# A recurrence of sigmoids cut into chunks of ten tokens: three column chains in place of two halves, fewer filler matmuls, a first sweep that begins a token later

## The chip, the cores and the metric

One core of one Trainium2 chip. Times are microseconds of the device for one launch, median of several runs; lower is better.

## The reference, cut to what matters

The model is a graph convolution block, an attention layer and a recurrent layer on 32 batches, 32 channels and 400 tokens. The change touches only the recurrent layer at the end:

```python
Wx = ((flat - mean) * rsqrt(var + 1e-5) * gamma + beta)      # normalised over all batches and tokens
Vt = V.T                                                     # V is 32x32 and orthogonal (from a QR)
def step(yt, wx_t):
    yt = sigmoid(wx_t + yt @ Vt)
    return (yt, yt)
y0 = zeros((B, H))
_, ys = lax.scan(step, y0, swapaxes(Wx, 0, 1))               # 400 tokens, one after the other
t = t + swapaxes(ys, 0, 1)
```

`gamma` and `beta` are drawn with a spread; everything is float32.

## The kernel before, in words

Layout. Four batches of 32 channels fill the 128 partitions, and there are G = 8 such groups, so a value of one token is 128 partitions x 8 columns. Matmul weights are block diagonal.

The recurrence is not run through 400 tokens. The sequence is cut into NC = 40 chunks of L = 10 tokens, and all chunks run side by side: one step takes token s of every chunk, 8 x 40 = 320 columns. A first sweep starts every chunk from a state of zero; since a state of zero needs no matmul, its first token is a sigmoid alone, and SKIP = 1 leaves out token 0, so it covers tokens 1 to 9. Its last states, moved by one chunk (`chain`, L833), start the second sweep of ten steps, which gives the output. A test (L881 to L890) then compares the last states of the two sweeps: if any of them differs by more than 2^-18 (MEET is its square), 39 further sweeps run. The profile shows none.

Within a sweep the 320 columns go as two halves h of 160 columns (groups 0 to 3 and 4 to 7), so that one half's matmul runs beside the other's sigmoid. For each step and half:

- VectorE has put `scl * ul + shf` (the normalised input) into a slot of PSUM ahead of time (`seed`, L829: 2 or 3 steps of one half in one instruction). PLACES = 9 slots for each half lie three to a bank in banks 4h to 4h+2.
- TensorE adds V to it (L1183; a float32 matmul is two pairs of LDWEIGHTS and MATMUL), and then runs a filler, a bf16 matmul of 256 columns into an unused bank (`fill`, L1173).
- ScalarE takes the sigmoid from the slot to `yb` (L587), which is the input of the next matmul of that half.

Each engine takes its instructions in program order, and on each the halves alternate: h0, h1, h0, h1. The semaphores are `seeded` (VectorE to TensorE), `pre` (TensorE to ScalarE), `y_ok` (ScalarE to TensorE and VectorE).

Ahead of the first step: the statistics over all tokens end with a small float32 matmul (L1176), two small ScalarE instructions (L579, L581), a table load for the sigmoid (L584), and `scl` and `shf` on VectorE (L822, L823). Beside them TensorE writes six banks once, so that the steps' matmuls can accumulate (`prime`, L1168, 480 columns each), and runs FILLS_FIRST = 10 fillers. The first token's sigmoid (L598) reads `ul` with `scl` and `shf` as scale and bias.

Between the sweeps VectorE moves the states (L836, once for each half), then copies the last states for the test (L852, all 320 columns), and ScalarE waits for this copy before the second sweep. During the second sweep VectorE adds the residual for each token in turn (L869, 320 columns), and seeds the slot of token 9 after token 3's sigmoid. The last token is added by halves (L874), and after each half SyncE issues two output DMAs of 400 KB (L339).

Of the kernel before, what the change touches and what calls it, by code (L numbers as in the profile page):

```python
# [42 lines left out]
NC = N // L  # L43
PLACES = 9
SKIP = 1
FILL = 256
FILLS_FIRST = 10
COLS = G * NC
HALF = COLS // 2
FULL = N // P  # L50
# [31 lines left out]
def build(nc, x_tok, x, consts, out):  # L82
    with ExitStack() as ctx:
# [16 lines left out]
        ka, kb, qa, qb = ([sb(f"{name}{h}", [P, NB, N], BF16) for h in range(2)] for name in ("ka", "kb", "qa", "qb"))  # L100
        ul = sb("ul", [P, 2, L, G // 2, NC])
        yb = sb("yb", [P, L + 1, G, NC])
# [56 lines left out]
        def col(n, w=1, rows=P):  # L159
# [4 lines left out]
        bn_s2, bn_h2 = col(19, 3), col(22, 3)  # L164
        mv, tot, nvar, lnv, rsv, scl, shf, okc = (
            col(25, 2), col(27, 2), *(col(n) for n in range(29, 35)))
        S_GC, S_Z, S_POST = 0, 1, 2
# [29 lines left out]
            sem(n) for n in ("bn_c", "bn_pe", "bn_act", "primed", "cmp_c", "cmp_pe", "flag_ok", "added"))  # L197
        start_ok = [sem("start_ok0"), sem("start_ok1")]
        seeded = [sem("seeded0"), sem("seeded1")]
        pre = [sem("pre0"), sem("pre1")]  # L200
        y_ok = [sem("y_ok0"), sem("y_ok1")]

# [3 lines left out]
        CREDIT_DMA = 16  # L206
        OUT_G = 2
        LOADED = 14 * 16
        WARM_FIRST, WARM = 10, 2
        SLOT = HALF  # L210
        PRIMED = 3 * SLOT
        PRIME_ORDER = (0, 4, 1, 5, 2, 6)
        FILL_BANK, SMALL_BANK = 3, 7
        LAST_STEP_ADDS = L + 1

# [12 lines left out]

        def step_slot(h, p):

            return ps[:, 4 * h + p // 3, SLOT * (p % 3):SLOT * (p % 3 + 1)]

        def seed_count(sweep, s):

            return s // 3 + 1 + (PLACES // 3 + 1) * sweep - 1 if sweep else (s - SKIP - 1) // 3 + 1

        def y_half(h, s):

            return yb[:, s, 4 * h:4 * h + 4, :].rearrange("p g c -> p (g c)")

# [28 lines left out]
        def _(sp):  # L269
# [65 lines left out]
            def store_output(sums):  # L335
                for h in range(2):
                    sp.wait_ge(added, LAST_STEP_ADDS * (sums - 1) + L + h)
                    for g in range(4 * h, 4 * h + 4, OUT_G):
                        sp.dma_start(out[g:g + OUT_G].rearrange("g p n -> p g n"),  # L339
                                     outs[:, g:g + OUT_G, :]).then_inc(out_done, 16)  # L340
                sp.wait_ge(out_done, 16 * (G // OUT_G) * sums)

# [57 lines left out]
        def _(act):  # L400
# [185 lines left out]
            def step(h, sweep, s):  # L586
                nc.scalar.activation(y_half(h, s + 1), step_slot(h, place(sweep, s)), ACT.Sigmoid).then_inc(y_ok[h], 1)  # L587
# [12 lines left out]
            for s in range(SKIP + 1, L):  # L600
                for h in range(2):
                    act.wait_ge(pre[h], s - SKIP)
                    step(h, 0, s)
# [9 lines left out]
        def _(dve):  # L613
# [150 lines left out]
            def project2(g, banks=NORM_BANKS):  # L764
                dve.wait_ge(wx_done, g + 1)
                dve.wait_ge(rs2_ready, g + 1)
                nc.vector.tensor_tensor(ul[:, g // 4, :, g % 4, :],  # L767
                                        ps[:, banks[1], 0:N].rearrange("p (c s) -> p s c", s=L),
                                        rs2.rearrange("p (c s) -> p s c", s=L), ALU.mult).then_inc(u2_ready, 1)

            def stats(g):
                dve.wait_ge(u2_ready, g + 1)
                nc.vector.bn_stats(stat[:, g, :], ul[:, g // 4, :, g % 4, :]).then_inc(stat_ready, 1)

# [32 lines left out]
            def blink(ins):  # L807
# [15 lines left out]
            blink(nc.vector.scalar_tensor_tensor(out=shf, in0=tot[:, 0:1], scalar=scl, in1=c_("beta"),  # L823
                                                 op0=ALU.mult, op1=ALU.add))

            def seed(h, sweep, lo, hi):

                o = SLOT * (place(sweep, lo) % 3)
                nc.vector.tensor_scalar(ps[:, 4 * h + place(sweep, lo) // 3, o:o + SLOT * (hi - lo)],  # L829
                                        ul[:, h, lo:hi, :, :].rearrange("p s g c -> p (s g c)"),  # L830
                                        scl, shf, ALU.mult, ALU.add).then_inc(seeded[h], 1)

            def chain(h, base):  # L833

                dve.wait_ge(y_ok[h], base)
                nc.vector.tensor_copy(yb[:, 0, 4 * h:4 * h + 4, 1:NC],  # L836
                                      yb[:, L, 4 * h:4 * h + 4, 0:NC - 1]).then_inc(start_ok[h], 1)

            FIRST = ((SKIP + 1, SKIP + 4), (SKIP + 4, SKIP + 7), (SKIP + 7, L))
            LATER = ((0, 3), (3, 6), (6, 9))  # L840

            for lo, hi in FIRST:
                for h in range(2):
                    dve.wait_ge(primed, 1 + PRIME_ORDER.index(4 * h + place(0, lo) // 3))
                    seed(h, 0, lo, hi)
            for lo, hi in LATER[:-1]:
                for h in range(2):
                    dve.wait_ge(y_ok[h], hi + 1)
                    seed(h, 1, lo, hi)
            for h in range(2):  # L850
                chain(h, L - SKIP)
            nc.vector.tensor_copy(ys, yb[:, L, :, :]).then_inc(cmp_c, 1)  # L852
            for h in range(2):
                seed(h, 1, *LATER[-1])

            def last_seeds(base):

                for h in range(2):
                    dve.wait_ge(y_ok[h], base + 3)
                    seed(h, 1, PLACES, L)  # L860

            def add_residual(base, seeding=False):

                for j in range(L - 1):
                    if seeding and j == 3:
                        last_seeds(base)
                    for h in range(2):
# [4 lines left out]
                for h in range(2):  # L872
                    dve.wait_ge(y_ok[h], base + L)
                    nc.vector.tensor_tensor(by_step(outs[:, 4 * h:4 * h + 4, :], L - 1),  # L874
                                            by_step(t0[:, 4 * h:4 * h + 4, :], L - 1),
                                            y_half(h, L), ALU.add).then_inc(added, 1)

# [12 lines left out]
            with dve.If(dve.value_load(flag[0:1, 0:1], min_val=0, max_val=1) != 0):  # L890
                with dve.Fori(0, NC - 1) as k:
                    for h in range(2):
# [4 lines left out]
                for h in range(2):  # L897
                    dve.wait_ge(y_ok[h], 2 * L - SKIP + L * (NC - 1))
                dve.wait_ge(out_done, 16 * (G // OUT_G))
                add_residual(2 * L - SKIP + L * (NC - 2))  # L900
# [3 lines left out]
        def _(pe):  # L904
# [277 lines left out]
            def step(h, sweep, s):  # L1182
                mm_(step_slot(h, place(sweep, s)), c_("vT"), y_half(h, s), start=False, stop=True,  # L1183
                    skip_group_check=True).then_inc(pre[h], 1)
                fill()

            def steps(sweep):
                for s in range(L):
                    for h in range(2):
                        pe.wait_ge(seeded[h], seed_count(1, s) + (PLACES // 3 + 1) * (sweep - 1))  # L1190
                        if s == 0:
# [5 lines left out]
            for s in range(SKIP + 1, L):  # L1197
                for h in range(2):
                    pe.wait_ge(seeded[h], seed_count(0, s))
# [111 lines left out]
```

## Time and profile before

| what | us |
|---|---|
| median of 3 runs | 222.96 (222.94 to 223.4) |
| span of the profiled execution | 221.9 |
| mean granted TensorE clock over it | 0.966 |
| the recurrence's first matmul starts, in that span | 195.38 |
| its last pair of matmuls ends | 213.97 |
| first output DMA is issued | 214.51 |

The span runs from the first instruction of the program to the last; the launch's own time for that one execution is not given, and the median of the runs is 1.0 above the span. In the profile PE is TensorE's matmuls, PEld its weight loads, DVE VectorE, ACT ScalarE, SP SyncE (SPq its issuing of DMAs). The end of a matmul is modelled, its start is not. PEclk is the granted TensorE clock: 1.00 is 2.4 GHz, 0.50 is 1.2 GHz.

### The profile page before, as it was taken

The page shows a single profiled execution, that of the slowest core. Times are in us where ns is not written, and L with a number is a line of the kernel's source. Part 1 is how long each engine was busy: PE and PEld are TensorE (multiplying, and loading weights), DVE is VectorE, ACT ScalarE, POOL GpSimd, SP SyncE. Part 2 cuts the span into 40 slices and gives each one's busy share as a digit, 9 for nine tenths or more (in the row PEclk, how much of TensorE's full clock was granted, in tenths as well). Part 3 has the DMA queues.
Part 4 walks back from the last instruction along what each step waited for, and adds up shares of the span by engine and source line. Part 5 has one row for each costly group of instructions (what it writes and reads, how often), then busy time and mean ns, then how long its engine had stood idle before and what let it go on. Part 6 is the DMA issues. An engine that isn't in the chain of part 4 may idle for free. (4 is left out here: it accounts for less than half of the span.)

```text
span 221.9 us, 3477 instructions
## 1 busy us (share of the span) xinstructions
PE 198.5 (89%) x1182; PEld 97.9 (44%) x1182; DVE 161.2 (73%) x294; ACT 169.1 (76%) x307; POOL 29.8 (13%) x44
## 2 busy tenths in 40 slices
PE   6858999999999869699999999999999997699950
PEld 6733655646546335123243434334343332376630
DVE  0559289989989926978685777859596865765980
ACT  4083798799599799988989989898989954445630
POOL 7000000450330160432020000101010000000000
PEclk9999999999999999979999999999999999579995
DMA  6940200357348050880627162443500000000016
GB/s 183 370 149 15 74 1 0 98 220 200 123 150 219 20 222 3 273 194 6 167 58 190 38 155 71 117 111 85 140 0 3 0 0 0 3 3 0 0 65 234
DMA packets 20229, 21.95 MB, mean 99 GB/s; under 512 B 2062, under 2 KB 17102, under 8 KB 20084
## 3 DMA queue, kind: packets, MB, share of 16 engines
q1 hardware_dynamic: 20212, 21.73, 33.5%
q8 instruction: 10, 0.16, 0.3%
q14 instruction: 7, 0.06, 0.1%
HBM read 14.74 MB, written 6.96 MB: 98 GB/s over the span
## 5 line engine op out<-in xcount | busy, mean ns | idle before, releaser
L508 ACT ACTIVATE arena<-ps 128x800 f32<-128x800 f32 (+1 forms) x56 | 44.6, 798 | 5.8 <-PE ps L1066 5.3
L515 ACT ACTIVATE arena<-arena 128x800 f32<-128x800 f32 (+1 forms) x56 | 46.5, 831 | 0.0
L1066 PE MATMUL ps<-qa,ka 128*128 128x400 bf16 (+1 forms) x128 | 35.4, 340 | 2.0 <-ACT arena L508 1.9
L1066 PE MATMUL ps<-qb,kb 96*128 96x400 bf16 (+1 forms) x128 | 35.4, 338 | 0.0
L742 DVE TENSOR_TENSOR psum<-arena 128x400 f32<-128x400 f32 x32 | 19.6, 612 | 14.3 <-ACT arena L515 14.3
L742 DVE TENSOR_TENSOR psum<-psum,arena 128x400 f32<-128x400 f32 x32 | 19.5, 608 | 6.0 <-ACT arena L515 4.6
L1066 PEld LDWEIGHTS ps<-qa,ka 128*128 128x128 bf16 (+1 forms) x128 | 10.4, 97 | 26.1 <-ACT arena L508 13.7
L1099 PE MATMUL ps<-arena,vb 128*32 128x400 f32 x192 | 21.6, 527 | 0.3 <-issue 0.3
L751 DVE RECIPROCAL arena<-ps 128x400 f32<-128x400 f32 x7 | 18.5, 2650 | 0.0
L661 DVE COPY arena<-arena 32x400 f32<-32x400 f32 x48 | 17.2, 358 | 0.9
L587 ACT ACTIVATE yb<-ps 128x160 f32<-128x160 f32 x36 | 10.9, 303 | 9.1 <-PE ps L1183 6.8
L1183 PE MATMUL ps<-yb,cst 128*128 128x160 f32 x72 | 17.1, 332 | 0.0
L967 PE MATMUL ps<-arena,cst 128*128 128x400 f32 x32 | 13.0, 528 | 3.3 <-DVE arena L661 3.3
L368 POOL TENSOR_TENSOR arena<-arena,cst 128x400 bf16<-128x400 f32 x4 | 5.0, 1248 | 71.5 <-ACT arena L476 61.7
L1066 PEld LDWEIGHTS ps<-qb,kb 96*128 96x128 bf16 (+1 forms) x128 | 10.4, 98 | 9.2 <-issue 5.2
L1183 PEld LDWEIGHTS ps<-yb,cst 128*128 128x128 f32 x72 | 11.2, 196 | 5.8 <-issue 4.0
L378 POOL COPY vb<-vst 128x384 f32 (+1 forms) x8 | 4.8, 595 | 60.9 <-PE ps L1095 60.9
L1173 PE MATMUL ps<-ka 128*128 128x256 bf16 x46 | 12.3, 308 | 0.0
L829 DVE TENSOR_SCALAR ps<-ul,small 128x480 f32<-128x480 f32 (+2 forms) x14 | 9.0, 702 | 3.6 <-ACT yb L587 3.6
L702 DVE TENSOR_TENSOR arena<-arena 128x400 bf16<-128x400 f32 x16 | 11.2, 741 | 0.0
L421 ACT ACTIVATE arena<-ps,small 96x400 f32<-96x400 f32 (+1 forms) x16 | 10.5, 675 | 0.9 <-PE ps L958 0.7
L679 DVE TENSOR_TENSOR arena<-ps,arena 128x400 f32<-128x400 f32 x8 | 4.2, 568 | 8.8 <-ACT arena L454 8.8
(148 smaller groups left out, 360.9 us busy)
## 6 DMA issues: line engine op xcount, KB each, us to landing
ka<-dk SPq DMA_DIRECT2D x32, 100.0 KB
qa<-dq SPq DMA_DIRECT2D x32, 100.0 KB
dk<-arena SPq DMA_DIRECT2D x8, 300.0 KB, 2.2
dq<-arena SPq DMA_DIRECT2D x8, 300.0 KB, 2.6
arena<-x_tok SPq DMA_DIRECT2D x4, 400.0 KB
t<-x SPq DMA_DIRECT2D x1, 1600.0 KB, 11.4
kb<-dk SPq DMA_DIRECT2D x16, 100.0 KB
qb<-dq SPq DMA_DIRECT2D x16, 100.0 KB
```

The costliest lines, as they stand in the source:

```text
L508: nc.scalar.activation(prob[par][:, lo:hi, :], ps[:, o:o + hi - lo, 0:N], ACT.Exp, scale=2.0).then_inc(e1_done, 1)
L515: nc.scalar.activation(p, p, ACT.Exp).then_inc(p_ready, 1)
L587: nc.scalar.activation(y_half(h, s + 1), step_slot(h, place(sweep, s)), ACT.Sigmoid).then_inc(y_ok[h], 1)
L661: last = nc.vector.tensor_copy(*tap_input(par, j, k))
L702: nc.vector.tensor_tensor(p[par][:, slots[2], :], r[par], p[par][:, slots[1], :], ALU.subtract).then_inc(parts_ready, 1)
L742: nc.vector.tensor_tensor(dst, a, prob[par][:, t, :], ALU.add).then_inc(part_sum, 1)
L751: nc.vector.reciprocal(rden, ps[:, 5, 0:N]).then_inc(rden_ready, 1)
L967: mm_(ps[:, 2 * par + 1, 0:N], cst[:, o + P * j:o + P * j + P], tap_in[par][j], start=(j == 0), stop=False)
L1066: last = mm_(ps[row:row + keys, bank, 0:N], kk[par][0:rows, b, o:o + keys], qq[par][0:rows, b, :], start=first, stop=not first, skip_group ...
L1099: mm_(ps[C * b:C * b + C, 4, 0:N], vb[:, par, P * k + C * b:P * k + C * b + C], prob[par][:, FULL * b + k, :], start=(k == 0), stop=False, ...
L1173: mm_(ps[:, FILL_BANK, 0:FILL], ka[0][:, 0, 0:P], ka[0][:, 0, 0:FILL], start=True, stop=True)
L1183: mm_(step_slot(h, place(sweep, s)), c_("vT"), y_half(h, s), start=False, stop=True, skip_group_check=True).then_inc(pre[h], 1)
```

## The change

The columns of the recurrence go as three chains of 3, 3 and 2 groups, that is 120, 120 and 80 columns, and every loop over h has three members. Each chain has two banks (2h and 2h+1) with four slots each (ROOM), PLACES = 8 slots in all; seeds are for 4 steps of one chain (2 or 3 at a sweep's end). The filler after each step's matmul goes, and of the ten fillers in front three stay. The first sweep starts at token 2 (SKIP = 2) from states of 0.5: an added float32 matmul of one column (V times ones) ahead of L1176 and an added VectorE instruction give the bias `shf_first = shf + 0.5 * V 1` for its first sigmoid. The output goes as three DMAs (600, 600, 400 KB) in place of four. The scaled input `ul` is laid out by token, group, chunk.

```diff
-PLACES = 9
-SKIP = 1
+PLACES = 8
+ROOM = 4
+SKIP = 2
-FILLS_FIRST = 10
+FILLS_FIRST = 3
-HALF = COLS // 2
+CHAINS = ((0, 3), (3, 6), (6, 8))
+WIDE = 3 * NC
-        PRIME_ORDER = (0, 4, 1, 5, 2, 6)
+        PRIMED = ROOM * WIDE
+        PRIME_ORDER = (0, 2, 4, 1, 3, 5)
 # SyncE
-                for h in range(2):
+                for h, (lo, hi) in enumerate(CHAINS):
                     sp.wait_ge(added, LAST_STEP_ADDS * (sums - 1) + L + h)
-                    for g in range(4 * h, 4 * h + 4, OUT_G):
-                        sp.dma_start(out[g:g + OUT_G].rearrange("g p n -> p g n"),
-                                     outs[:, g:g + OUT_G, :]).then_inc(out_done, 16)
+                    sp.dma_start(out[lo:hi].rearrange("g p n -> p g n"), outs[:, lo:hi, :]).then_inc(out_done, 16)
 # ScalarE
-            for h in range(2):
-                act.wait_ge(bn_c, 5)
-                nc.scalar.activation(y_half(h, SKIP + 1), ul[:, h, SKIP, :, :].rearrange("p g c -> p (g c)"),
-                                     ACT.Sigmoid, bias=shf, scale=scl).then_inc(y_ok[h], 1)
+            act.wait_ge(bn_c, 6)
+            for h, (lo, hi) in enumerate(CHAINS):
+                nc.scalar.activation(y_part(h, SKIP + 1), ul[:, SKIP, lo:hi, :].rearrange("p g c -> p (g c)"),
+                                     ACT.Sigmoid, bias=shf_first, scale=scl).then_inc(y_ok[h], 1)
 # VectorE
+            blink(nc.vector.scalar_tensor_tensor(out=shf_first, in0=ps[:, SMALL_BANK, 8:9], scalar=0.5, in1=shf,
+                                                 op0=ALU.mult, op1=ALU.add))
-            FIRST = ((SKIP + 1, SKIP + 4), (SKIP + 4, SKIP + 7), (SKIP + 7, L))
-            LATER = ((0, 3), (3, 6), (6, 9))
+            FIRST = ((SKIP + 1, SKIP + 1 + ROOM), (SKIP + 1 + ROOM, L))
+            LATER = ((0, ROOM), (ROOM, 2 * ROOM))
-            for lo, hi in LATER[:-1]:
-                for h in range(2):
-                    dve.wait_ge(y_ok[h], hi + 1)
-                    seed(h, 1, lo, hi)
+            for h in range(len(CHAINS)):
+                dve.wait_ge(y_ok[h], ROOM + 1)
+                seed(h, 1, *LATER[0])
 ...
-                    if seeding and j == 3:
+                    if seeding and j == ROOM:
                         last_seeds(base)
 # TensorE
+            mm_(ps[:, SMALL_BANK, 8:9], c_("vT"), c_("ones")[:, 0:1], start=True, stop=True)
             mm_(ps[:, SMALL_BANK, 0:2], c_("avg4"), mv, start=True, stop=True).then_inc(bn_pe, 1)
 ...
             def step(h, sweep, s):
-                mm_(step_slot(h, place(sweep, s)), c_("vT"), y_half(h, s), start=False, stop=True,
+                mm_(step_slot(h, place(sweep, s)), c_("vT"), y_part(h, s), start=False, stop=True,
                     skip_group_check=True).then_inc(pre[h], 1)
-                fill()
```

## Rows read from the trace of the kernel before

**Rows 1.** Chain of waits ahead of the first step: start us, us, what
```profile
193.46 2.13 PE ps L1173 x10
```
**Rows 2.** Timeline of TensorE, same stretch: start us, us, engine, line, operation, tiles, shapes
```profile
190.68 0.35 PE L1176 MATMUL ps<-small,cst 128*128 128x2 f32 x1
190.90 2.56 PE L1168 MATMUL ps<-ka 128*128 128x480 bf16 x6
...
195.38 0.47 PE L1183 MATMUL ps<-yb,cst 128*128 128x160 f32 x1
195.65 0.47 PE L1183 MATMUL ps<-yb,cst 128*128 128x160 f32 x1
```
**Rows 3.** Timeline of ScalarE and VectorE, same stretch
```profile
192.07 1.28 ACT L584 ACT_TABLE_LOAD   x1
192.35 0.22 DVE L823 SCALAR_TENSOR_TENSOR small<-small,cst 128x1 f32<-128x1 f32 x1
192.61 3.85 DVE L829 TENSOR_SCALAR ps<-ul,small 128x480 f32<-128x480 f32 x6
193.37 0.93 ACT L598 ACTIVATE yb<-ul,small 128x160 f32<-128x160 f32 x2
```
**Rows 4.** Groups by line, 189 to 222 us: count | busy us, mean ns | idle before, releaser
```profile
L829 DVE TENSOR_SCALAR ps<-ul,small 128x480 f32<-128x480 f32 x10 | 7.2, 774 | 3.6 <-ACT yb L587 3.6
```
**Rows 5.** Timeline, one cycle of h0 in the second sweep
```profile
206.04 0.30 PEld L1183 LDWEIGHTS ps<-yb,cst 128*128 128x128 f32 x2 [0.23 <-issue]
206.61 0.30 ACT L587 ACTIVATE yb<-ps 128x160 f32<-128x160 f32 x1 [0.27 <-PE ps L1183]
207.03 0.30 PEld L1183 LDWEIGHTS ps<-yb,cst 128*128 128x128 f32 x2 [0.23 <-issue]
```
**Rows 6.** Timeline, output DMAs, and two steps ahead of them on VectorE
```profile
213.41 0.73 DVE L869 TENSOR_TENSOR outs<-t,yb 128x320 f32<-128x320 f32 x1 [0.25 <-ACT yb L587]
214.06 0.77 DVE L874 TENSOR_TENSOR outs<-t,yb 128x160 f32<-128x160 f32 x2
214.51 2.59 SPq L339 DMA_DIRECT2D out<-outs  x4
```
**Rows 7.** Busy time: PE, PEld, DVE, ACT, POOL, PEclk, DMA share, GB/s
```profile
219.00:219.50 0.50, 0.00 (x0) 0.00 (x0) 0.00 (x0) 0.00 (x0) 0.00 (x0) 0.50 1.03 394
```
**Rows 8.** Timeline, h0's pairs: tokens 3 and 9 of sweep one, 1 and 9 of sweep two
```profile
196.72 0.44 PE L1183 MATMUL ps<-yb,cst 128*128 128x160 f32 x2
202.69 0.30 PE L1183 MATMUL ps<-yb,cst 128*128 128x160 f32 x1
205.07 0.37 PE L1183 MATMUL ps<-yb,cst 128*128 128x160 f32 x1
213.03 0.37 PE L1183 MATMUL ps<-yb,cst 128*128 128x160 f32 x1
```
**Rows 9.** Timeline of ScalarE: one activation at two widths
```profile
174.34 0.84 ACT L508 ACTIVATE arena<-ps 128x800 f32<-128x800 f32 x1
...
176.19 0.50 ACT L508 ACTIVATE arena<-ps 128x400 f32<-128x400 f32 x1 [0.25 <-PE ps L1066]
```
**Rows 10.** Timeline, two float32 matmuls of 128 columns in a stream
```profile
11.90 0.39 PE L1036 MATMUL ps<-cst 128*128 128x128 f32 x2
12.13 0.39 PE L1037 MATMUL ps<-cst 128*128 128x128 f32 x2
```
**Rows 11.** Timeline of VectorE between the sweeps
```profile
204.27 0.32 DVE L852 COPY ys<-yb 128x320 f32<-128x320 f32 x1
```
**Rows 12.** Busy time, columns as in rows 7, with the granted clock (PEclk)
```profile
80.50:83.90 3.40, 1.97 (x6) 1.24 (x7) 1.05 (x2) 3.00 (x6) 1.18 (x2) 1.00 0.11 37
186.30:189.70 3.40, 1.34 (x4) 0.40 (x3) 1.76 (x3) 1.13 (x2) 0.00 (x0) 1.00 0.00 0
189.70:193.10 3.40, 2.65 (x8) 1.31 (x9) 2.20 (x9) 1.53 (x3) 0.00 (x0) 0.50 0.01 2
193.10:196.50 3.40, 3.40 (x16) 2.57 (x15) 3.35 (x6) 1.49 (x4) 0.00 (x0) 0.50 0.01 2
```

More of the change, by code:

```diff
@@ L164, in build @@
         bn_s2, bn_h2 = col(19, 3), col(22, 3)
-        mv, tot, nvar, lnv, rsv, scl, shf, okc = (
-            col(25, 2), col(27, 2), *(col(n) for n in range(29, 35)))
+        mv, tot, nvar, lnv, rsv, scl, shf, okc, shf_first = (
+            col(25, 2), col(27, 2), *(col(n) for n in range(29, 36)))
         S_GC, S_Z, S_POST = 0, 1, 2
@@ L197, in build @@
             sem(n) for n in ("bn_c", "bn_pe", "bn_act", "primed", "cmp_c", "cmp_pe", "flag_ok", "added"))
[L198 to L201, printed above, removed]
+        start_ok = [sem(f"start_ok{h}") for h in range(len(CHAINS))]
+        seeded = [sem(f"seeded{h}") for h in range(len(CHAINS))]
+        pre = [sem(f"pre{h}") for h in range(len(CHAINS))]
+        y_ok = [sem(f"y_ok{h}") for h in range(len(CHAINS))]
         CREDIT = 2
@@ L227, in place, with step_slot, y_part @@
             return s - SKIP - 1 if sweep == 0 else s % PLACES
-        def step_slot(h, p):
-            return ps[:, 4 * h + p // 3, SLOT * (p % 3):SLOT * (p % 3 + 1)]
+        def step_slot(h, p, steps=1):
+            width = (CHAINS[h][1] - CHAINS[h][0]) * NC
+            return ps[:, 2 * h + p // ROOM, width * (p % ROOM):width * (p % ROOM + steps)]
         def seed_count(sweep, s):
-            return s // 3 + 1 + (PLACES // 3 + 1) * sweep - 1 if sweep else (s - SKIP - 1) // 3 + 1
-        def y_half(h, s):
-            return yb[:, s, 4 * h:4 * h + 4, :].rearrange("p g c -> p (g c)")
+            return s // ROOM + (PLACES // ROOM + 1) * sweep if sweep else (s - SKIP - 1) // ROOM + 1
+        def y_part(h, s):
+            return yb[:, s, CHAINS[h][0]:CHAINS[h][1], :].rearrange("p g c -> p (g c)")
         def apart(eng):
@@ L824, in _ @@
                                                  op0=ALU.mult, op1=ALU.add))
+            blink(nc.vector.scalar_tensor_tensor(out=shf_first, in0=ps[:, SMALL_BANK, 8:9], scalar=0.5, in1=shf,
+                                                 op0=ALU.mult, op1=ALU.add))
             def seed(h, sweep, lo, hi):
[L828 to L830 removed]
+                nc.vector.tensor_scalar(step_slot(h, place(sweep, lo), hi - lo).rearrange("p (s n) -> p s n", s=hi - lo),
+                                        ul[:, lo:hi, CHAINS[h][0]:CHAINS[h][1], :].rearrange("p s g c -> p s (g c)"),
@@ L842, in _ @@
+            FIRST = ((SKIP + 1, SKIP + 1 + ROOM), (SKIP + 1 + ROOM, L))
+            LATER = ((0, ROOM), (ROOM, 2 * ROOM))
             for lo, hi in FIRST:
-                for h in range(2):
-                    dve.wait_ge(primed, 1 + PRIME_ORDER.index(4 * h + place(0, lo) // 3))
+                for h in range(len(CHAINS)):
+                    dve.wait_ge(primed, 1 + PRIME_ORDER.index(2 * h + place(0, lo) // ROOM))
                     seed(h, 0, lo, hi)
-            for lo, hi in LATER[:-1]:
-                for h in range(2):
-                    dve.wait_ge(y_ok[h], hi + 1)
-                    seed(h, 1, lo, hi)
@@ L850, in _ @@
-            for h in range(2):
+            for h in range(len(CHAINS)):
+                dve.wait_ge(y_ok[h], ROOM + 1)
+                seed(h, 1, *LATER[0])
+            for h in range(len(CHAINS)):
                 chain(h, L - SKIP)
             nc.vector.tensor_copy(ys, yb[:, L, :, :]).then_inc(cmp_c, 1)
-            for h in range(2):
-                seed(h, 1, *LATER[-1])
+            for h in range(len(CHAINS)):
+                seed(h, 1, *LATER[1])
             def last_seeds(base):
-                for h in range(2):
-                    dve.wait_ge(y_ok[h], base + 3)
+                for h in range(len(CHAINS)):
+                    dve.wait_ge(y_ok[h], base + ROOM)
@@ L864, in add_residual @@
                 for j in range(L - 1):
-                    if seeding and j == 3:
+                    if seeding and j == ROOM:
                         last_seeds(base)
-                    for h in range(2):
+                    for h in range(len(CHAINS)):
                         dve.wait_ge(y_ok[h], base + j + 1)
@@ L871, in add_residual @@
                                             ALU.add).then_inc(added, 1)
-                for h in range(2):
+                for h, (lo, hi) in enumerate(CHAINS):
                     dve.wait_ge(y_ok[h], base + L)
-                    nc.vector.tensor_tensor(by_step(outs[:, 4 * h:4 * h + 4, :], L - 1),
-                                            by_step(t0[:, 4 * h:4 * h + 4, :], L - 1),
-                                            y_half(h, L), ALU.add).then_inc(added, 1)
+                    nc.vector.tensor_tensor(by_step(outs[:, lo:hi, :], L - 1), by_step(t0[:, lo:hi, :], L - 1),
+                                            y_part(h, L), ALU.add).then_inc(added, 1)
             add_residual(L - SKIP, seeding=True)
@@ L891, in _ @@
                 with dve.Fori(0, NC - 1) as k:
-                    for h in range(2):
+                    for h in range(len(CHAINS)):
                         chain(h, 2 * L - SKIP + L * k)
@@ L896, in _ @@
                     last_seeds(2 * L - SKIP + L * k)
-                for h in range(2):
+                for h in range(len(CHAINS)):
                     dve.wait_ge(y_ok[h], 2 * L - SKIP + L * (NC - 1))
-                dve.wait_ge(out_done, 16 * (G // OUT_G))
+                dve.wait_ge(out_done, 16 * len(CHAINS))
                 add_residual(2 * L - SKIP + L * (NC - 2))
@@ L1182, in step @@
             def step(h, sweep, s):
-                mm_(step_slot(h, place(sweep, s)), c_("vT"), y_half(h, s), start=False, stop=True,
+                mm_(step_slot(h, place(sweep, s)), c_("vT"), y_part(h, s), start=False, stop=True,
                     skip_group_check=True).then_inc(pre[h], 1)
-                fill()
             def steps(sweep):
                 for s in range(L):
-                    for h in range(2):
-                        pe.wait_ge(seeded[h], seed_count(1, s) + (PLACES // 3 + 1) * (sweep - 1))
+                    for h in range(len(CHAINS)):
+                        pe.wait_ge(seeded[h], seed_count(1, s) + (PLACES // ROOM + 1) * (sweep - 1))
                         if s == 0:
@@ L1197, in _ @@
             for s in range(SKIP + 1, L):
-                for h in range(2):
+                for h in range(len(CHAINS)):
                     pe.wait_ge(seeded[h], seed_count(0, s))
```

23 lines of the change are left out of this document (10 added, 13 removed).

## The prediction

> **What bounds the kernel now.** I read the chain of waits first, then the timeline along it, then busy time by stretch for the clock and the DMAs. Ahead of the first step the chain runs through TensorE's fillers [rows 1]. The timelines [rows 2, 3] show that this is padding: h0's first sigmoid begins at 193.37 and ends near 193.9 (two overlap in 0.93), its seed is done at 192.61 + 0.77 = 193.38 [rows 4], yet its first matmul starts at 195.38, after ten fillers. So 1.4 us of the front is filler on the path.
>
> In the steps nobody is full; each half is bound by its own round trip [rows 5]: weight load at 206.04, both matmuls, sigmoid at 206.61 (0.57 after the load) for 0.30, next weight load at 207.03 (0.12 after its end). Sum 0.99. The fillers lie in the gaps. Eighteen such steps run: eight in the first sweep, ten in the second.
>
> The end is DMA: the first of four is issued at 214.51 [rows 6], and while they run the DMA share is 1.03 at 394 GB/s [rows 7]. 1.64 MB at this rate is 4.2 us of the 7.4 from the first issue to the span's end; the rest is start, landing and closing. So what counts is when the first output DMA is issued.
>
> **The change part by part.** I follow chain 0 against h0 by the start of its pairs: 195.38 for token 2, 196.72 for token 3, 202.69 for token 9, then 205.07 and 213.03 for tokens 1 and 9 of the second sweep [rows 2, 8].
>
> *Front, later part.* The added float32 matmul (V times ones) stands ahead of L1176, which everything behind waits for. One MATMUL of L1176 starts at 190.68 and the next instruction's at 190.90 [rows 2]: 0.22 each at the half clock, two of them 0.44. That goes on the path: statistics, two small activations, table load and sigmoids all start 0.44 later. Bounds: 0, were it started earlier than the wait lets it, and 0.58, both matmuls unpipelined. The added VectorE instruction, 0.22 like L823 plus a gap of 0.04, ends inside the table load of 1.28 [rows 3] and costs the sigmoid nothing; the seeds begin 0.26 later beyond the 0.44, at 193.31.
>
> *Front, earlier part.* The table load then ends at 193.80. The first sigmoid with 120 columns takes 0.51 less 0.03 (40 columns at 0.85 ns: 400 columns more cost L508 0.84 - 0.50 [rows 9]) and ends at 194.28. Chain 0's seed (480 columns, 0.77) ends at 194.08. TensorE's primes end near 193.7 and three fillers at 0.213 each (2.13 for ten [rows 1]) near 194.3: still hidden. Weight load 0.12 after the sigmoid, so the first pair starts at about 194.45, for token 3.
>
> *Half-clock steps.* Chains 1 and 2 wait for their seeds (194.8, 195.3), and at half clock two 120-column float32 MATMULs and loads take about 0.22 each, 0.43 per pair: three pairs make a step of 1.28. Walking them through: pairs start at 194.45, 194.9 and 195.4. Chain 0's first pair is through at about 195.1 (0.23 to the second MATMUL, 0.2 of columns, 0.2 of drain), its sigmoid at 195.4, but chain 2's pair holds TensorE until 195.85, where chain 0's token 4 starts. That pair ends at 196.45, the sigmoid at 196.77, and as the clock returns at 196.5 as now, token 5 starts at 196.92. Now h0's token 5 starts two steps of 0.995 after 196.72, at 198.71. Ahead: 1.79. In it are the token no longer computed (about 1.0 to 1.3), the fillers, and the 0.44 lost.
>
> *Warm steps.* With 120 columns a round trip loses 40 columns in the second matmul and in the sigmoid. A float32 MATMUL takes two cycles a column (160 columns in the 0.27 from 195.38 to 195.65, at 1.2 GHz [rows 2]), so 40 are 0.033 at 2.4 GHz; the sigmoid's 40 are 0.033. The first matmul I let save nothing, since the second waits for its own weights (0.03 more if it does save). 0.995 - 0.066 = 0.93. Does it fit? TensorE: in a stream, pairs of 128 columns start 0.23 apart [rows 10], and I take the same for 120 and 80, since loads set it: three make 0.69. ScalarE: 0.27 + 0.27 + 0.24 = 0.78 without overlap. Both are under 0.93, so the latency still binds. A price by columns alone would make the three 0.53, which changes nothing. Bounds for a step: 0.86 (the 80-column trip, if it could lead) and 1.00 (the wider interleaving costs what the columns save); I take 0.93, the arithmetic above. Four steps to token 9 of the first sweep save 0.25: ahead by 2.04. Eight steps in the second save 0.50.
>
> *Between the sweeps.* h0 needs 2.38 from token 9 to token 1, of which about 0.2 is the state copy and 0.2 ScalarE's wait for the 320-column copy of 0.32 [rows 11]. With three chains that copy stands behind three state copies, and the last of these waits for chain 2's last sigmoid. Chain 0's pair for token 9 starts at 200.65, its sigmoid ends at 201.43, those of chains 1 and 2 at 201.86 and 202.03. State copies of 0.2 end at 201.66, 202.09 and 202.28, the copy of all columns at about 202.52. Chain 0's next pair starts at 201.81 and is through at 202.3; its sigmoid waits until 202.55, and the sigmoids of chains 1 and 2, queued behind it, are due at 202.76 and 203.0 and lose nothing. So 1.16 to the first pair and 1.16 to the second, 2.32, ahead by 2.10, with the eight steps 2.60. Bounds: 2.0 and 2.9.
>
> The seeds for tokens 0 to 3 now wait for chain 0's fifth sigmoid (198.6) and end by 200.6, ahead of their use at 201.8: nothing.
>
> *VectorE behind it* is the engine that could come late. Six seeds run in 3.85 [rows 3], 0.64 each in mean, so three make 1.9; four additions of 0.65 (213.41 to 214.06 [rows 6]) 2.6; the last seeds 1.2. From the copy's end, 202.5, this ends near 208.2; chain 0 needs its slot for token 8 at 209.5. 1.3 us to spare, so nothing.
>
> *End.* Now from h0's last pair to the first DMA it is 1.48. The full-width addition for token 8 waits for the last chain, then 0.65, then chain 0's own addition of 0.38 (0.42 less 40 columns): 1.37. Ahead by 2.7. The output's bytes are the same and each engine of the DMA is full, so three issues for four gain 0 (0.2 at most).
>
> Sum: 195.38 to 194.45 and on, in all 2.7. The profiled span of 221.94 becomes 219.2; the median lies 1.0 above the span, which surrounds both: 222.96 - 2.7 = **220.3**.
>
> **The clock** is what I trust least, because what fed TensorE in the gaps is removed. In the trace the granted clock fell to 0.50 at 189.7, after 3.4 us in which PE was busy for 1.34, and stayed there over the next stretch, busy for 2.65; it rose at 196.5, after a stretch in which it was busy throughout [rows 12]. From 80.5 to 83.9 it was busy for 1.97 and the clock stayed at 1.00. After the change the steps at full clock hold 0.53 us of columns in 0.93 (320 columns, two MATMULs of two cycles), plus loads and drains; in the stretch ahead of 196.5 the primes, three fillers and the cold pairs leave gaps of perhaps 0.3 us. I expect the clock to come back and to stay.
> The Trainium skill speaks against the change here: "TensorE: Matmul & The Clock Gate", section "A second HAM failure mode: psum-queue depth-cycling", tells of a kernel whose TensorE paused briefly between groups of matmuls often enough that its clock went back and forth between the two levels. By that rule the steps here would run at 1.2 GHz in part or throughout; by the row from 80.5 they would not. It is the first rival.
>
> **Rivals.**
> 1. *The clock doesn't come back, or falls in the steps.* For it: the filler went from every gap, and the stretch of 2.65 busy did not raise the clock. Against: the row from 80.5, and cold pairs fill TensorE nearly wholly. Price: at half clock a step is set by three pairs of 0.43, 1.28 in place of 0.93. For 14 steps that is 4.9: 225.2, slower than before. It decides once more than 8 of the steps are cold (8 x 0.35 = 2.8). Chance 0.15. If the rise comes only one such stretch later (2.7 steps, 0.95): 221.3, chance 0.10.
> 2. *Three chains don't fit.* In-order engines alternate three, and TensorE's queue must pass a wait, two loads and two matmuls for each; were it 1.0 per step, 12 warm steps lose 0.07 each: 221.2. For it: a load is issued 0.12 after its sigmoid even now. Chance 0.09.
> 3. *The test between the sweeps fails.* Taking the reference's recurrence on its own inputs in double precision, the largest difference of a chunk's last state between the sweeps is 1.2e-6 now; with eight tokens from 0.5 it is 3.0e-6, against the limit of 2^-18 = 3.8e-6. It passes with a fifth to spare. Otherwise 39 sweeps of 9.7 follow, 380 us: 600. Chance 0.03.
>
> **How the numbers follow.** The forecast's own case has 0.63, from 219.6 to 221.0: the added matmul's bounds (-0.4, +0.1), the step between 0.90 and 0.96 (12 x 0.03 = 0.4 each way), the copies 0.3. With the delayed clock and rival 2 the range is 219.5 to 222.3; it leaves out the cold clock and the failed test, 0.18, and a little below. A measurement tells 0.2%, 0.45 us, from nothing. Faster: 0.63 + 0.10 + 0.09, less 0.04 for combinations of them: 0.78. Slower: 0.15 + 0.03 = 0.18. Same: 0.04.
>
> **What would show it.** PEclk 1.00 from about 196.5 until the last pair. First pair of the recurrence near 194.4, for a table load ending near 193.8. Chain 0's pairs 0.93 apart, TensorE's loads in groups of six. First output DMA near 211.8, with the DMA share at 1.0 behind it. Wrong: clock at 0.50 in the steps, pairs at 1.0 apart or more, VectorE's last seeds later than the matmul that waits for them, or instructions of the 39 further sweeps.

## The result, and the profile after

The changed kernel takes 221.73 us in the median of 20 executions (220.54 to 223.88), the kernel before 223.00 in 20 beside it (221.42 to 225.61). The ratio is 0.9944, interval 0.9917 to 0.9971: 1.3 us faster by the medians, where 2.7 was forecast. A second set, of 6 executions of the changed kernel and 23 of the kernel before, gave 221.43 against 223.70, ratio 0.990 (0.9847 to 0.9952): 2.3 faster by the medians. Both kernels vary from execution to execution by 1% and more; the ratios leave out executions more than 1.5% above a kernel's fastest, most of them of the kernel before, so they can understate the gain. The means of the first set are 223.30 and 221.86, of the second 223.68 and 221.54. Over all 112 executions of the kernel before and all 26 of the changed one, which were not all made side by side, they are 223.68 and 221.79: 1.9 apart.

The profiled execution of the changed kernel has a span of 219.2 and took 221.07. The 39 further sweeps did not run.

The chain of waits ahead of the first step (start us, us, what) has lost its primes and fillers [rows 1]; it now goes through the table load and the first sigmoid:

```profile
190.73 0.38 PE ps L1174 x2
191.11 0.24 PE ps L1175 x2
...
192.37 1.28 ACT L583
193.66 0.49 ACT yb L597
```

TensorE's timeline answers to [rows 2]. Its clock is at 2.4 GHz here: the primes take 1.38 for six (2.56 before), and TensorE then waits 1.40 for the sigmoid:

```profile
190.97 0.36 PE L1175 MATMUL ps<-small,cst 128*128 128x2 f32 x2
191.19 1.38 PE L1166 MATMUL ps<-ka 128*128 128x480 bf16 x6
192.41 0.49 PE L1171 MATMUL ps<-ka 128*128 128x256 bf16 x3
194.29 6.41 PE L1182 MATMUL ps<-yb,cst 128*128 128x120 f32 x33 [1.40 <-ACT yb L597]
```

Busy time by stretch (PE, PEld, DVE, ACT, POOL, PEclk, DMA share, GB/s) answers to [rows 12]. The clock did not fall ahead of L1175; it fell at 196.3, inside the steps, and came back at 199.7 (PEclk, the last number but two):

```profile
189.50:192.80 3.30, 2.07 (x13) 1.25 (x13) 2.12 (x8) 0.93 (x3) 0.00 (x0) 1.00 0.00 0
192.80:196.20 3.40, 2.00 (x13) 1.58 (x12) 3.33 (x8) 3.09 (x9) 0.00 (x0) 1.00 0.02 5
196.20:199.60 3.40, 3.40 (x18) 3.40 (x17) 1.36 (x3) 1.96 (x8) 0.00 (x0) 0.51 0.02 5
206.00:209.40 3.40, 3.36 (x24) 2.87 (x23) 3.40 (x7) 2.49 (x12) 0.00 (x0) 1.00 0.00 0
```

Chain 0's pairs start 0.90 apart at full clock (206.72, 207.63, 208.53, 209.44, 210.34) and 1.33 and 1.28 apart between 196.3 and 199.7 (196.28, 197.61, 198.89). Between the sweeps and at the end the timeline has, against [rows 11, 6]:

```profile
201.74 0.68 DVE L837 COPY yb<-yb 128x117 f32<-128x117 f32 x3 [1.11 <-ACT yb L586]
202.34 0.32 DVE L851 COPY ys<-yb 128x320 f32<-128x320 f32 x1
202.69 0.68 ACT L586 ACTIVATE yb<-ps 128x120 f32<-128x120 f32 x3 [0.50 <-DVE ys L851]
...
207.42 0.52 DVE L829 TENSOR_SCALAR ps<-ul,small 128x240 f32<-128x240 f32 x1
207.85 0.43 DVE L829 TENSOR_SCALAR ps<-ul,small 128x160 f32<-128x160 f32 x1
...
210.76 0.72 DVE L868 TENSOR_TENSOR outs<-t,yb 128x320 f32<-128x320 f32 x1
211.39 0.82 DVE L873 TENSOR_TENSOR outs<-t,yb 128x120 f32<-128x120 f32 x3
211.77 2.03 SPq L339 DMA_DIRECT2D out<-outs  x3
```

The first output DMA (SPq, the issuing of DMAs), forecast at 211.8, is issued at 211.77, and the span, forecast at 219.2, is 219.2. So the two profiles differ by just the 2.7 of the forecast, and the medians of the first set by half of it. That is the question of the experiments.

### The profile page after: what moved, and what is told of

The parts are those of the page before. It is cut to its first block and busy times, and to the rows that moved or that the text cites. A ratio compares the mean times of both kernels' runs of the same rounds, so it can differ in the third digit from the quotient of the medians.

```text
span 219.2 us, 3489 instructions
## 1 busy us (share of the span) xinstructions
PE 193.8 (88%) x1171; PEld 98.4 (45%) x1171; DVE 160.7 (73%) x298; ACT 170.3 (78%) x323; POOL 29.8 (14%) x44
## 5 line engine op out<-in xcount | busy, mean ns | idle before, releaser
L1182 PE MATMUL ps<-yb,cst 128*128 128x120 f32 (+1 forms) x102 | 16.6, 309 | 1.7 <-ACT yb L597 1.4
L1182 PEld LDWEIGHTS ps<-yb,cst 128*128 128x128 f32 x102 | 14.7, 212 | 3.7 <-DVE ps L829 1.8
L586 ACT ACTIVATE yb<-ps 128x120 f32<-128x120 f32 (+1 forms) x51 | 11.9, 260 | 4.8 <-PE ps L1182 3.7
L438 ACT ACTIVATE t<-arena,small 128x400 f32<-128x400 f32 x8 | 4.8, 630 | 7.6 <-DVE arena L670 7.4
L416 ACT ACTIVATE arena<-ps,small 128x400 f32<-128x400 f32 x8 | 5.4, 685 | 6.6 <-PE ps L951 6.6
```

The lines of the kernel that those rows point to most:

```text
L586: nc.scalar.activation(y_part(h, s + 1), step_slot(h, place(sweep, s)), ACT.Sigmoid).then_inc(y_ok[h], 1)
L1182: mm_(step_slot(h, place(sweep, s)), c_("vT"), y_part(h, s), start=False, stop=True, skip_group_check=True).then_inc(pre[h], 1)
```

## The experiments

I split each profile at two marks: the start of the matmul of avg4 (L1176 before, L1175 after; here "the mark") and the first output DMA. In the first two profiles: start to mark 190.45 and 190.97, mark to DMA 24.06 and 20.80, DMA to end 7.43 and 7.43.

Each launch also gives the mean granted clock of its execution. Every profile has one stretch of half clock in the first part or the middle, mostly near 94 us, and one at the end. With these two alone the mean is 0.978 or more (0.98 to 0.987 in most); below that, there was a further stretch. The number does not say where it lay. The medians of the kernel before also differ from one set of executions to the next (223.00, 223.49, 223.70, 223.38, 224.31), so that kernels of different sets are best compared through the kernel before beside them.

**Both kernels again.** No edit.

> The kernel before, unchanged, for a second profile of it. Theory A (the two profiled executions were not typical ones: the half-clock stretches fall elsewhere from execution to execution): the time from L1176 to the first output DMA, 24.06 in the first profile, comes out otherwise here, by 0.5 or more, and with it the place where the granted clock is 0.50. Theory B (the profile of before was typical, and what is lost is lost in executions of the changed kernel that the one profile of it does not show): 24.0 to 24.1 again, clock at half from 189.7 to 196.5 again, and launch time minus span 1.0.

> The changed kernel, unchanged, for a second profile of it. Theory A: from L1176 to the first output DMA 21.05 was one draw; another place of the half-clock stretch gives 20.0 to 23. Theory B: 22 or more, with half clock in the steps for two stretches of 3.4 or more. A third theory, that the part ahead of L1176 (the same in both kernels) varies by a microsecond and hides the difference: the start of L1176 moves by 0.5 or more against 190.73.

Busy time of the kernel before in its second profile, mark to DMA in the first line:

```profile
191.44:213.54 22.10, 20.70 (x126) 14.00 (x126) 17.24 (x33) 13.66 (x41) 0.00 (x0) 1.00 0.01 1
188.10:191.40 3.30, 0.53 (x2) 0.00 (x0) 2.02 (x4) 1.03 (x2) 0.00 (x0) 1.00 0.00 0
```

and of the changed kernel:

```profile
191.74:212.51 20.77, 18.31 (x115) 15.51 (x114) 16.51 (x36) 14.63 (x57) 0.00 (x0) 0.92 0.01 2
193.60:197.00 3.40, 2.00 (x13) 1.61 (x12) 3.33 (x8) 3.08 (x9) 0.00 (x0) 1.00 0.02 5
197.00:200.40 3.40, 3.40 (x18) 3.40 (x18) 1.35 (x3) 1.92 (x8) 0.00 (x0) 0.50 0.02 5
```

TensorE in the second profile of the kernel before, ten fillers and the first pair of matmuls:

```profile
192.90 1.25 PE L1173 MATMUL ps<-ka 128*128 128x256 bf16 x10
194.82 0.51 PE L1183 MATMUL ps<-yb,cst 128*128 128x160 f32 x2 [0.67 <-ACT yb L598]
```

Theory A (another execution, another place of the half clock) holds for the kernel before: 22.10 at full clock, in place of 24.06 with half clock at 189.7 to 196.5. Its first profile had caught an execution that loses 1.96 there. The changed kernel shows 20.77 and its half clock in the same place again. Of the executions of the kernel before, 36 of 92 have a mean clock of 0.978 or more (222.63 in the mean; the other 56: 224.49); of the changed kernel 1 of 26. The 20 executions of the kernel before in the first set have no clock on record. The mark itself moved, too, to 191.44 and 191.74: the part ahead of it, to which the change adds only the 0.24 of the new matmul, varies by a microsecond and more (over all fourteen profiles from 190.45 to 192.59). The third theory, that this hides the difference, is true of single executions.

**The wait for the statistics filled, in both kernels.**

```diff
             project2(G - 1, LAST_BANKS[G - 1])
+            for _ in range(26):
+                mm_(ps[:, 4, 0:FILL], ka[0][:, 0, 0:P], ka[0][:, 0, 0:FILL], start=True, stop=True)
```

> The kernel before with 26 more fillers (256 columns, bf16) right behind the last projection, in the 2.8 us in which TensorE waits for the statistics. Theory A: the clock stays at 1.00 from there to the last step, primes and fillers run at 0.20 and 0.107, the first step starts as soon as the sigmoid is there (3.6 us after L1176 in place of 4.9), and L1176 to first DMA is 22.4. The median falls by the average cost of the half-clock stretches in the kernel before, 0.5 to 1.5 us, and the times of its runs lie closer together. Theory B: no stretch in before costs anything, the median moves by under 0.3.

> The changed kernel with the same 26 fillers in the same place. Theory A: L1176 to first DMA 19.8 to 20.0, and 2.3 to 2.6 below the kernel before with the same fillers; against the changed kernel 1 to 2 lower, since its steps pay for a half-clock stretch by 0.38 a step and nothing in them covers it. If in its steps, without fillers, the clock falls all the same: half clock in a stretch of 3.4 within the steps, 21 or more, and the gain stays at 1 us against the kernel before with the same fillers.

Kernel before, mark to DMA and the stretch ahead of the mark:

```profile
190.81:212.90 22.09, 20.70 (x127) 13.99 (x126) 17.26 (x33) 13.67 (x41) 0.00 (x0) 1.00 0.01 1
187.40:190.80 3.40, 3.40 (x28) 2.55 (x26) 2.03 (x4) 1.09 (x2) 0.00 (x0) 1.00 0.02 5
```

Changed kernel:

```profile
192.56:212.28 19.72, 17.03 (x115) 13.97 (x114) 16.57 (x36) 14.28 (x57) 0.00 (x0) 1.00 0.01 2
192.90:196.30 3.40, 2.00 (x13) 1.05 (x10) 2.53 (x8) 2.83 (x6) 0.00 (x0) 1.00 0.02 5
```

The kernel before: median 222.94 against 223.70, mean clock 0.978 or more in 9 of 12 executions, and 22.09 as expected of the full clock (22.4 was 0.3 too much). The changed kernel without half clock takes 19.72: that is its own price, 2.38 less than 22.10, and the half-clock stretch in its steps costs 20.77 - 19.72 = 1.05. Its median is 221.23 (6 executions), hardly below the 221.43 of the changed kernel beside it, where 1 to 2 less was expected. The mark lay late in its profile (192.56), and 3 of 6 still have a further stretch; how much each takes back is open.

**The fillers, one place at a time.** In this order:

```diff
 # changed kernel, ten in front
-FILLS_FIRST = 3
+FILLS_FIRST = 10
 # changed kernel, behind the step's matmul
+                fill()
 # kernel before, three in front
-FILLS_FIRST = 10
+FILLS_FIRST = 3
 # kernel before, behind the step's matmul
-                fill()
```

> The changed kernel with ten fillers in front in place of three, none behind steps. Theory C (the half-clock stretch in its steps, from 196.3 in its profile, comes from the 1.4 us in which TensorE now waits ahead of the first step, 192.9 to 194.3): the clock stays at 1.00 through the steps, L1175 to first DMA 19.7 to 19.9 in place of 20.8, the median about 1 lower. Rival D (it comes from the missing fillers behind the steps): the stretch is there as before, 20.8, median unmoved.

> The changed kernel with a filler behind each step's matmul again, three in front. Theory D: no half clock in the steps. Theory C: it comes all the same. Either way a full-clock step is then set by TensorE, three pairs of 0.223 and three fillers of 0.107, 0.99 in place of 0.90: 12 or more of them cost 1.1 to 1.4, L1175 to first DMA 21.0 without a half-clock stretch, 22 or more with one.

> The kernel before with three fillers in front in place of ten, a filler behind each step as it was. Theory C: the wait ahead of the first step now brings half clock into its steps in about every execution; steps at half clock 1.2 to 1.5 in place of 1.0 for one stretch, L1176 to first DMA 22.6 to 23.3 against 22.1. Rival D: the fillers behind steps keep the clock, 22.1, or less where the clock had fallen ahead of L1176 (24.06 becomes 22.9).

> The kernel before with no filler behind steps, ten in front. Theory C: clock as in the kernel before, steps 0.99 (0.96 where a filler had held up h1), L1176 to first DMA 22.0 to 22.1, median within 0.5 of the kernel before. Rival D: half clock in the steps in about every execution, 22.6 or more.

Mark to DMA in the four, in this order; of the first also the half clock, which here fell ahead of the mark:

```profile
192.48:213.81 21.33, 20.51 (x121) 16.54 (x121) 16.34 (x35) 14.68 (x57) 0.00 (x0) 0.87 0.01 2
191.30:194.70 3.40, 2.67 (x9) 1.59 (x10) 1.78 (x9) 1.11 (x3) 0.00 (x0) 0.50 0.00 0
194.70:198.10 3.40, 3.40 (x16) 2.43 (x15) 3.36 (x7) 1.92 (x5) 0.00 (x0) 0.50 0.02 5
```

```profile
190.95:211.54 20.59, 18.80 (x166) 16.95 (x165) 16.86 (x36) 16.05 (x57) 0.00 (x0) 1.00 0.01 2
```

```profile
190.84:212.90 22.06, 19.93 (x119) 13.30 (x119) 17.23 (x33) 13.63 (x41) 0.00 (x0) 1.00 0.00 1
```

```profile
191.46:214.20 22.74, 18.31 (x90) 13.02 (x90) 17.25 (x33) 13.13 (x41) 0.00 (x0) 0.92 0.01 1
192.60:196.00 3.40, 3.40 (x16) 2.38 (x15) 2.97 (x6) 2.44 (x5) 0.00 (x0) 0.50 0.02 5
```

Medians, with the ratio to the kernel before beside them and its interval:

| kernel | median | ratio | executions at 0.978 or more |
|---|---|---|---|
| changed | 221.73, 221.43 | 0.9944, 0.990 | 1 of 26 |
| changed, ten in front | 221.28 | 0.9931 (0.9893 to 0.9969) | 4 of 11 |
| changed, filler behind steps | 221.41 | 0.9932 (0.9895 to 0.9969) | 8 of 12 |
| before | 223.49, 223.70, 223.38, 224.31 | | 36 of 92 |
| before, three in front | 222.91 | 1.0042 (1.0003 to 1.0082) | 6 of 12 |
| before, none behind steps | 223.37 | 1.0036 (0.9997 to 1.0076) | 2 of 12 |

Neither theory C (the wait ahead of the first step loses the clock) nor D (the missing fillers behind the steps do) stands alone. With fillers behind the steps the most executions of the changed kernel are without a further stretch (8 of 12 against 1 of 26), with ten in front some (4 of 11); I cannot say more from eleven. In the kernel before three in front in place of ten take 22.06 in place of 22.10: at full clock seven fillers are worth 0.04. The ratio has that kernel 0.4% slower than the kernel before (1.0042), the means have it 0.1 us faster (223.50 against 223.60), so I read no difference from either. What theory D gains is paid back: in the changed kernel a step with three fillers is 0.94 to 0.95 in place of 0.90 (I had expected 0.99), and 20.59 is hardly less than 20.77.

The first and the last profile lost the clock in a third place. With ten in front, half clock lay over the primes, all ten fillers and the start of the first step, as in the first profile of the kernel before: the first pair starts 4.92 behind the mark in place of 3.32, and 21.33 is 1.6 more than 19.72. With none behind the steps it lay over the last two primes, the fillers and about half of the first step (first pair 3.90 behind the mark in place of 3.38, first step 1.23 in place of 1.00: 22.74). All its further steps, without any filler, ran at full clock and 1.00 apart, so steps of two halves without fillers do not by themselves lose it. The last count decides nothing: its profile has two more half-clock stretches, of 3.4 each, in the first 25 us, far ahead of the recurrence.

**The token and the chains, one at a time.** The kernel before with the first sweep from token 2 and states of 0.5; the changed kernel with it from token 1 and states of zero, the opposite edit.

```diff
-SKIP = 1
+SKIP = 2
 ...
-                act.wait_ge(bn_c, 5)
+                act.wait_ge(bn_c, 6)
-                                     ACT.Sigmoid, bias=shf, scale=scl).then_inc(y_ok[h], 1)
+                                     ACT.Sigmoid, bias=shf_first, scale=scl).then_inc(y_ok[h], 1)
+            blink(nc.vector.scalar_tensor_tensor(out=shf_first, in0=ps[:, SMALL_BANK, 8:9], scalar=0.5, in1=shf,
+                                                 op0=ALU.mult, op1=ALU.add))
+            mm_(ps[:, SMALL_BANK, 8:9], c_("vT"), c_("ones")[:, 0:1], start=True, stop=True)
```

> The kernel before with one part of the change alone: the first sweep starts at token 2 from 0.5, with the added matmul and bias; two halves, all fillers. Where no half-clock stretch falls behind L1176 the kernel before needs 22.10 from L1176 (the matmul of avg4) to the first output DMA; a step less takes 0.995; the added matmul lies ahead of that mark, so 21.1, and 0.22 to 0.26 is lost ahead of it (from the end of the statistics to the mark). Median 0.7 to 0.8 below the kernel before. A rival, that the clock lottery grows worse: median unmoved.

> The changed kernel without that part: three chains of 120, 120 and 80, three fillers in front and none behind steps, but the first sweep from token 1 and a state of zero. With no half-clock stretch L1176 to first output DMA is 19.72 (the changed kernel with the gap filled) plus 0.90, 20.6; with one stretch in the steps 21.7. Theory C/D (the missing fillers make such a stretch fall in about every execution): half clock in its steps in the profile, 21.7. Median 0.3 to 1.0 below the kernel before, by the columns and fillers alone.

The first: mark to DMA by busy time, and VectorE between the sweeps:

```profile
192.59:214.03 21.44, 19.67 (x122) 13.31 (x121) 16.82 (x34) 13.05 (x39) 0.00 (x0) 1.00 0.01 2
```

```profile
201.82 1.46 DVE L831 TENSOR_SCALAR ps<-ul,small 128x480 f32<-128x480 f32 x2 [1.53 <-ACT yb L587]
203.18 0.38 DVE L838 COPY yb<-yb 128x156 f32<-128x156 f32 x2
```

The second, mark to DMA, and its half clock in the steps:

```profile
191.63:213.19 21.56, 19.17 (x119) 16.62 (x119) 16.86 (x35) 15.65 (x60) 0.00 (x0) 0.92 0.01 2
197.20:200.60 3.40, 3.40 (x18) 3.40 (x17) 1.77 (x4) 2.01 (x9) 0.00 (x0) 0.50 0.02 5
```

One token less in two halves gives 0.66 (22.10 to 21.44), not 0.995: the second seeds (1.46) now stand ahead of the state copies on VectorE, and h0's trip between the sweeps is 1.63 in place of 1.27. In three chains the same token gives 0.79 (21.56 against 20.77, both with one half-clock stretch in the steps), nearer to the 0.90 of a step; between the sweeps chain 0's pairs are 1.18 apart in both, since only one bank of seeds stands there. The chains with their fewer fillers are worth 22.10 - 20.5 = 1.6 at full clock, where 20.5 is 21.56 less the 1.05 of the stretch; this last figure is worked out, not run.

Four profiles at full clock split this further: 22.10 before, 21.44 with the token, 20.59 with the three chains and all step fillers (three in front, worth the 0.04 above), 19.72 without the step fillers. They are one profile each. So the token gives 0.66, the chains 0.85, and the fillers behind the steps cost 0.87 once there are three chains. In two halves they cost next to nothing: the steps are 1.00 with them and without.

Medians: 222.80 (ratio 0.9957, 0.991 to 1.0004) and 222.44 (0.9892, 0.9849 to 0.9935), the kernel before beside them 224.31. Both lie further below it than I expected (0.7 to 0.8 and 0.3 to 1.0), but the first ratio does not tell its kernel from the kernel before.

**A version from the findings.** V times ones goes ahead of the wait for the statistics, 24 fillers into that wait, 16 ahead of the steps; the second version has one filler a step besides, behind chain 2.

```diff
             project2(G - 1, LAST_BANKS[G - 1])
+            mm_(ps[:, SMALL_BANK, 8:9], c_("vT"), c_("ones")[:, 0:1], start=True, stop=True)
+            for _ in range(24):
+                mm_(ps[:, 4, 0:FILL], ka[0][:, 0, 0:P], ka[0][:, 0, 0:FILL], start=True, stop=True)
-            mm_(ps[:, SMALL_BANK, 8:9], c_("vT"), c_("ones")[:, 0:1], start=True, stop=True)
-FILLS_FIRST = 3
+FILLS_FIRST = 16
 # second version only, behind the step's matmul
+                if h == len(CHAINS) - 1:
+                    fill()
```

> A version that may beat both: the changed kernel with V times ones moved ahead of the wait for the statistics, 24 fillers in that wait, 16 in front of the steps (they fill the wait for the sigmoid, 192.4 to 194.2, at full clock) and none behind steps. Theory C: full clock from L1175 to the end in nearly every execution, avg4 matmul to first output DMA 19.7, steps 0.90, and median 1.0 to 1.5 below the changed kernel. Theory D: half clock still falls into the steps in some executions, as nothing fills them: the median gains 0.5 or less.

> The same with one filler in each step, behind chain 2's matmul. TensorE then has three pairs of 0.223 and one filler of 0.107, 0.78 of the step's 0.90, so the step is 0.90 to 0.92. Theory D: this one keeps the clock where the version without step fillers loses it, the median is lower than that one's by 0.3 to 1. Theory C: both keep it, and this one is 0 to 0.3 slower.

Busy time from mark to DMA in the first version, then in the second:

```profile
191.69:211.47 19.78, 18.53 (x126) 15.38 (x126) 16.74 (x36) 14.37 (x57) 0.00 (x0) 1.00 0.01 2
```

```profile
192.38:212.19 19.81, 19.17 (x143) 15.56 (x143) 16.73 (x36) 14.21 (x57) 0.00 (x0) 1.00 0.01 2
```

Both profiles have full clock from the mark to the last step, and the one filler a step costs nothing: 19.81. Medians 221.43 and 220.80 against 224.31 (ratios to the kernel before 0.9891, 0.9842 to 0.994, and 0.9829, 0.9775 to 0.9882). Both beat the kernel before. Against the changed kernel they were not timed side by side, and by the ratios to the kernel before (0.9944 and 0.990) only the second is likely ahead, from 6 executions; the 1.0 to 1.5 expected of the first did not show. 3 of 6 executions of each are under 0.978. That of the second version's profile is one of these, and its further half clock lies at 7.4 and 17.7 us, so such a count need not be about the recurrence; whether the fillers keep its clock in every execution isn't shown.

## Why the prediction was right or wrong

**The steps of the sum held, in the profile, but its exact hit was luck.** Added matmul: 0.44 forecast, 0.24 measured (190.73 to 190.97), since the clock was full there. Full-clock step: 0.93 forecast, 0.90 measured; the first matmul's columns save their 0.03 as well, which I had named as the bound. Half-clock step: 1.28 forecast, 1.28 measured. Between the sweeps: 2.32 forecast, 1.18 + 0.98 = 2.16 measured. VectorE's last seeds: end near 208.2 forecast, 208.28 measured, and the matmul for token 8 starts at 209.44, as said not late. Last pair to first DMA: 1.37 forecast, 1.43 measured. Three DMAs for four gain nothing: 7.43 and 7.43.

Along the path the misses have both signs and cancel. Start of the matmul of avg4: 190.97 for 190.89, with 0.28 later statistics against 0.20 less for the added matmul. From there to the first pair: 3.32 for 3.56. To token 9 of the first sweep: 6.66 for 6.20, since half clock lies here and I had it end at 196.5. Between the sweeps 0.16 less, the eight steps of the second 0.23 less, the end 0.06 more. Sum: 0.03 less than forecast. Without the half clock in the steps the changed kernel's profile would have come out about 1.05 below the forecast, as worked out from 20.77 and 19.72.

**What failed is the step from the profile to the median.** I wrote that "the median lies 1.0 above the span, which surrounds both". Launch time less span is 1.73 to 1.93 in every execution since (mean 1.81), so the profiled execution of before, whose own launch time isn't on record, took about 223.8 and was 0.8 above the median of its set (222.96, and 223.00 with all 20); that of the changed kernel, at 221.07, was 0.66 below its own. Together that is the missing 1.4. So 1.0 was no property of the launch: it was 1.8 less 0.8, a pair of one execution and one median that do not belong together. Part of the miss is the first set itself: against the mean of all 112 executions of the kernel before, 223.68, the profiled one is only 0.1 above, and by all executions the gain is 1.9, not 1.3. What is left is the changed kernel's profiled execution, 0.7 below its mean of 221.79.

**The term that failed is "1.4 us of the front is filler on the path".** It holds at half clock only. The profile showed half clock from 189.7 to 196.5 over the very fillers and primes that I had called padding. At full clock those ten fillers take 1.07 and are hidden: the second profile has its first pair at 194.82, 3.38 behind the mark, in place of 4.93, and three fillers in place of ten then gain 0.04 (22.10 to 22.06). So most of the gain that I gave to the fillers exists only in executions that have half clock over them. How many of the 56 under 0.978 have it there isn't known.

**The clock was mis-sized on the other side as well.** I expected it "to come back and to stay", and the sum put a later fall at nothing. It had not fallen in front, and it fell in the steps, in both profiles, for one stretch: 1.05. That is the first rival in a small version (about 3 steps of 1.28 where it wanted more than 8), worth 1.05 and not 4.9. By the mean clocks a further stretch is the usual case (25 of 26); that it lies there in all of them is not shown. Ahead of the fall, from 192.8 to 196.2, PE was busy for 2.00. My row from 80.5, busy for 1.97 at kept clock, did not decide it; with the gap filled, 192.9 to 196.3 had the same 2.00 and the clock stayed, so the busy time of that row alone does not tell these cases apart.
The Trainium skill, "TensorE: Matmul & The Clock Gate", section "A second HAM failure mode: psum-queue depth-cycling", tells of such a return to the lower level. The trace agrees in kind only: one stretch of 3.4 at half clock in the steps, and not a going back and forth.

**The balance of typical executions.** Mark to DMA 22.10 to 20.77 is 1.33, less 0.24 ahead of the mark: 1.1 from the usual execution of the changed kernel to the kernel before at full clock; to one with half clock over its fillers, 24.06 - 20.80 - 0.24 = 3.0. The kernel before is of both kinds, and the gains of the two sets, 1.3 and 2.3 by the medians and 1.4 and 2.1 by the means, lie between.

**The other rivals.** Three chains fit: 0.90 at full clock. The further sweeps ran in no profile, and no launch came near 600; how much the test has to spare was not measured.

**Open.** What moves the mark by 2 us between profiles of nearly the same upstream code was not tried; nor whether a version exists in which no execution loses the clock, nor what decides in which executions it falls. Why the first set shows 1.3 and the second 2.3 isn't known either; their intervals overlap.

## What to carry to other kernels

Before building a sum on one profile, place that execution in the spread of its own runs: take launch time less span from any other execution, and ask which stall in the profile belongs to that execution alone and which to the program. A filler that lies on the path at half clock may be free at full clock, so price an edit at both levels. And when fillers are removed, look where the clock falls next, in the work itself or in a wait ahead of it.

## What the runs showed of the hardware that I had not expected

The same program had its half-clock stretch over the fillers, or none there, from one execution to the next; in the two profiles that is 24.06 against 22.10. Executions of the kernel before with a mean clock under 0.978 are 1.9 longer in the mean (224.5 against 222.6), wherever their stretch lay. A float32 pair of MATMULs whose first load had only just been issued started 0.18 apart with 120 columns and 0.21 with 160, at full clock and with the same weights, so the gap is not set by the weight load alone. The table load ended at 193.65 and the first sigmoid started at 193.66.
